# A four-layer graph network kernel: where the next block's rows of x are loaded, which PSUM bank its transposes use, and when dense blocks may start

## The reference

```
edge_index = stack([src, dst])
x = _layernorm(x + _L0(x, edge_attr_16, src, dst, W1, W2, attn, bias))
x = _layernorm(x + _L1(x, edge_index, edge_weight, ...))
x = _layernorm(x + _L2(x, edge_index, W, b))
x = _layernorm(x + _L3(x, src, dst, edge_weight, 100000))

_L1:  e = exp(scores - seg_max[dst]); att = e / segment_sum(e, dst)[dst]
      out = segment_sum(att * (alpha * phys + (1 - alpha) * neur), dst)
      h = _layernorm(gelu(out) + x, ln1_g, ln1_b)
      m = gelu(h @ mlp_w1.T + mlp_b1) @ mlp_w2.T + mlp_b2
      return _layernorm(m + h, ln2_g, ln2_b)
_L3:  y = segment_sum(value[:, None] * x[col], row)
```

## Time and profile before

| | us |
|---|---|
| time, median of 3 runs | 3338.48 (3337.09 to 3351.1) |
| the profiled execution: its own time | 3352.47 |
| its span | 3350.7 |
| PE, DVE, ACT, POOL busy | 2159.2, 1627.2, 1632.0, 2055.5 |

### The profile page before, as it was taken

One profiled execution on the slowest core, in us unless ns is written; L12 is line 12 of the kernel. 1 busy time (PEld: TensorE's weight loads), 2 busy tenths in 40 slices (PEclk: granted clock), 3 DMA queues, 4 the chain that ended last, 5 costly groups with the idle time before them and its releaser, 6 DMA issues. The chain is left out here.

```text
span 3350.7 us, 28393 instructions
## 1 busy us (share of the span) xinstructions
PE 2159.2 (64%) x9124; PEld 1081.8 (32%) x9124; DVE 1627.2 (49%) x3065; ACT 1632.0 (49%) x2292; POOL 2055.5 (61%) x1609
## 2 busy tenths in 40 slices
PE   6885777687787888888885744778777730012221
PEld 3432333265333336334333633333332210001210
DVE  5873899837878673443332676332233310012221
ACT  4763566434677672777773333656567720001110
POOL 6888888600488810466657888688800048788887
PEclk9997898769999896999997656888899965555555
DMA  2221222106322211244347342111111101112221
GB/s 57 63 67 43 54 56 53 48 21 191 89 46 43 43 37 47 79 104 106 105 102 160 82 110 69 44 37 38 37 52 38 38 23 14 14 31 57 62 56 26
DMA packets 251594, 204.24 MB, mean 61 GB/s; under 512 B 182627, under 2 KB 192167, under 8 KB 251446
## 3 DMA queue, kind: packets, MB, share of 16 engines
q1 hardware_dynamic: 164998, 154.80, 16.3%
q0 software_dynamic: 83200, 47.29, 8.7%
q10 hardware_dynamic: 3248, 0.34, 0.1%
HBM read 133.83 MB, written 79.64 MB: 64 GB/s over the span
## 5 line engine op out<-in xcount | busy, mean ns | idle before, releaser
L810 PE MATMUL ps<-wk 127*64 127x125 f32 x1200 | 121.0, 367 | 559.0 <-DVE wk L795 558.0
L2172 POOL DMA_INDIRECT stab<-wk,rank_i x200 | 243.1, 1215 | 313.5 <-issue 247.8
L483 ACT ACTIVATE b_s<-ps,vec 128x512 f32<-128x512 f32 (+1 forms) x444 | 297.1, 682 | 125.7 <-PE ps L480 71.4
L2169 POOL DMA_INDIRECT u<-x2tab,dpos_i x200 | 278.0, 1390 | 79.6 <-issue 77.8
L2169 POOL DMA_INDIRECT u<-x3tab,src_i x200 | 258.4, 1292 | 72.3 <-issue 72.3
L2169 POOL DMA_INDIRECT u<-in_x_dram,dst_i x200 | 263.9, 1320 | 61.0 <-issue 57.6
L2169 POOL DMA_INDIRECT u<-in_x_dram,src_i x200 | 249.3, 1246 | 73.5 <-issue 69.2
L810 PEld LDWEIGHTS ps<-wk 127*64 127x64 f32 x1200 | 96.3, 191 | 580.7 <-DVE wk L795 576.7
L2172 POOL DMA_INDIRECT out_dram<-e_c,dst_i x72 | 89.4, 1242 | 309.2 <-issue 309.2
L840 ACT ACTIVATE e_a<-ps 128x500 f32<-128x500 f32 x75 | 44.0, 586 | 456.7 <-PE ps L810 452.3
L2169 POOL DMA_INDIRECT e_b<-x0tab,dpos_i x72 | 91.7, 1274 | 244.0 <-issue 244.0
(11 more groups left out here) (416 smaller groups left out, 5653.5 us busy)
## 6 DMA issues: line engine op xcount, KB each, us to landing
b_s<-in_x_dram SPq DMA_DIRECT2D x98, 256.0 KB
out_dram<-b_gl SPq DMA_DIRECT2D x98, 256.0 KB
wk<-dlist SPq DMA_DIRECT2D x50, 500.0 KB
wk<-slist SPq DMA_DIRECT2D x50, 500.0 KB
u<-stab SPq DMA_DIRECT2D x25, 510.0 KB
x2none<-b_gl SPq DMA_DIRECT2D x25, 250.0 KB
wk<-x2none SPq DMA_DIRECT2D x25, 240.0 KB
x2tab<-wk SPq DMA_DIRECT2D x25, 240.0 KB
```

The lines of the kernel that those rows point to most:

```text
L483: return nc.scalar.activation(b_s[l][:, 0:w], (pA, pB)[n][l][:, 0:w], ACT.Abs_reciprocal_sqrt, bias=col(EPSV))
L810: last_a = nc.tensor.matmul(e0[64 * (k % 2):64 * (k % 2) + 64, P * (k // 2):P * (k // 2) + P], msg[n % 2][0:P + 2, D * k:D * k + D], sr[n ...
L2169: pool.indirect_dma_start(out=o, out_offset=None, in_=tab, in_offset=at(ix), **kw).then_inc(s, 16)
L2172: pool.indirect_dma_start(out=tab, out_offset=at(ix), in_=a, in_offset=None, bounds_check=rows_n - 1, oob_is_err=False).then_inc(s, 16)
```

## The change

It has four parts. (1) The load of a dense block's rows of x goes to columns 512 to 1023 of the gelu buffer, and waits for the `w2` matmuls of the job before it on the lane (`mlp_pe{l}`), no longer for that job's `rows`. (2) The head of every job changes banks: `t` transposes into `pB`, `u` reads `pB`, the centred rows stand in `pA`, and the mean of squares in `pB`. `t` waits for the last reciprocal root of the job before (`rstds{l}`), `u` or `x` for its `rows` (`rows_ps{l}`), and the first matmul into `pA` for its `out` (`rows_out{l}`). In the plan the lane is given back at `r5` (dense) or `r4` (`src`, `dst`), no longer at `out`. (3) The plan starts no dense block while one of two spans is open: from the first `u3` step to the first `src` head, and from `lay` 1's step `b10` to the head of `dst` group 2. (4) The planner also counts loads of ScalarE's table for the reciprocal root, prefers a step that needs no new table among those ready at the same time, and counts an engine's slowness and table load when it chooses between ACT and DVE for `u` and `out`.

```diff
-            unit(("src", g), 1, "t pe .5 +lane;x act 1.2;s pe 2.2;r act .7;h dve .9;" + MLP + "rows pe .5;out act|dve .7 -lane",
+            unit(("src", g), 1, "t pe .5 +lane;x act 1.2;s pe 2.2;r act .7;h dve .9;" + LAST_MLP + "rows pe .5;out act|dve .7",
...
-                 "sq5 act .75;j5 pe 1.2;r5 act .7;o dve .75;rows pe .5;out act|dve .7 -lane", [(("dense", n - 1), "t", 0)] if n else ())
+                 "sq5 act .75;j5 pe 1.2;r5 act .7 -lane;o dve .75;rows pe .5;out act|dve .7", [(("dense", n - 1), "t", 0)] if n else ())
...
-        TABLES = {"gelu": 1, "g": 1, "exp": 2}
+        TABLES = {"gelu": 1, "g": 1, "exp": 2, "r": 3, "r3": 3, "r4": 3, "r5": 3, "rs": 3, "rst": 3}
...
-        GRACE = .2
+        GRACE, X_IN, SAME_TABLE = .1, 6.0, 0.0
+        HOLD = ((("u3", 0, "t"), ("src", 0, "t")), (("lay", 1, "b10"), ("dst", 2, "t")))
...
+                        if key[0] == "dense" and any(a in end and z not in end for a, z in HOLD):
+                            t = 1e6
...
 dense_pe
             if m:
-                pe.wait_ge(S(f"rows_out{l}"), m)
+                pe.wait_ge(S(f"rstds{l}"), c)
...
-                last_t = nc.tensor.transpose(pA[l][:, 128 * q:128 * q + 128], b_s[l][:, 128 * q:128 * q + 128], ident[:, :])
+                last_t = nc.tensor.transpose(pB[l][:, 128 * q:128 * q + 128], b_gl[l][:, 512 + 128 * q:640 + 128 * q], ident[:, :])
...
             pe.wait_ge(S(f"head_u{l}"), before(l, m, dense=1) + 1)
-            nc.tensor.matmul(pB[l], blk_c[:, :], b_h[l][:, :], start=True, stop=True).then_inc(S(f"head_c{l}"), 1)
+            if m:
+                pe.wait_ge(S(f"rows_out{l}"), m)
+            nc.tensor.matmul(pA[l], blk_c[:, :], b_h[l][:, :], start=True, stop=True).then_inc(S(f"head_c{l}"), 1)
...
 dense_sp
-            yield max(t["t"] - 6, lane_jobs[l][m - 1][0]["rows"] + 1.2 if m else 0)
+            yield lane_jobs[l][m - 1][0]["w2"] + 2.4 if m else t["t"] - 6
             if m:
-                sp.wait_ge(S(f"rows_ps{l}"), m)
-            sp.dma_start(b_s[l][:, :], x[dense_row(n):dense_row(n) + NB, :].rearrange("(p t) d -> p (t d)", p=128)).then_inc(
+                sp.wait_ge(S(f"mlp_pe{l}"), 3 * m - 1)
...
+            sp.dma_start(b_gl[l][:, 512:1024], x[dense_row(n):dense_row(n) + NB, :].rearrange("(p t) d -> p (t d)", p=128)).then_inc(
                 S(f"x_in{l}"), 16)
```

More of the change, by code:

```diff
@@ L191, in unit @@
             order.append(key)
[L193 to L194 removed]
+        MLP = ("w1 pe 1.3;gelu act 1.1;w2 pe 2.1;sq3 act .7;j3 pe 1.2;r3 act .7;mt dve .75;d pe 1.2;v dve .75;sq4 act .65;"
+               "j4 pe 1.2;r4 act .7{};x2 dve .7;")
+        LAST_MLP = MLP.format(" -lane")
+        MLP = MLP.format("")
         LANDED, STORED, EDGES_IN = 1.8, 4.5, 5.0
@@ L257, in gnn_resnorm_kernel @@
             sums_unit(NG + g, "msg dve 1.4;same dve 1.2;t pe .5 +lane;x act .6;a pe 2.2;ag act 1;o pe 1.2;g act .6;c pe 2.3;sq act .7;"
-                      "j pe 1.2;r act .7;h dve .75;" + MLP + "rows pe .5;out dve 1.3 -lane",
+                      "j pe 1.2;r act .7;h dve .75;" + LAST_MLP + "rows pe .5;out dve 1.3",
                       [(("lay", 1), "copy", CARRIED if g == 0 else 0)] + [(("xd1", g), "mul", 0)],
@@ L351, in make_plan, with lane_at, slow, switch @@
                     open_if(key, name)
+            def lane_at(l, key):
+                return max(lane_free[l], x_free[l] if key[0] == "dense" else 0.0)
+            def slow(eng, t):
+                return next((f for a, z, f in BUSY if a <= t < z), 1.0) if eng == "dve" else 1.0
+            def switch(eng, name):
+                return 1.28 if eng == "act" and TABLES.get(name, table[0]) != table[0] else 0.0
             def start(eng, key, name):
@@ L373, in make_plan @@
                     first = min(c[0] for c in cand)
-                    pick = min((units[s_[0]]["rank"], t, s_, eng) for t, s_ in cand if t <= first + GRACE)
+                    wait = max(GRACE, SAME_TABLE) if eng == "act" else GRACE
+                    pick = min((switch(eng, s_[1]), t > first + GRACE, units[s_[0]]["rank"], t, s_, eng)
+                               for t, s_ in cand if t <= first + wait)[2:]
                     if best is None or pick[1] < best[1]:
@@ L378, in make_plan @@
                 _, engs, us, takes, gives, _ = units[key]["steps"][name]
-                on[key[0], key[1], name] = eng
-                if eng == "dve":
-                    us *= next((f for a, z, f in BUSY if a <= t < z), 1.0)
-                if eng == "act" and TABLES.get(name, 0) != table[0]:
-                    table[0] = TABLES.get(name, 0)
-                    us += 1.28
+                on[key][name] = eng
+                if "|" not in engs:
+                    us = us * slow(eng, t) + switch(eng, name)
+                if eng == "act":
+                    table[0] = TABLES.get(name, table[0])
                 for e in engs.split("|"):
@@ L394, in make_plan @@
                     if r == "lane":
-                        l = min(LANES, key=lambda k: max(lane_free[k], lane_rows[k] + 6 if key[0] == "dense" else 0.0))
+                        l = min(LANES, key=lambda k: lane_at(k, key))
                         lane_of[key] = l
                         jobs[l].append((key, t))
-                        lane_free[l] = 1e9
+                        lane_free[l] = x_free[l] = 1e9
+                        names_ = list(units[key]["steps"])
+                        names_ = names_[names_.index("t"):]
+                        for k, p in ((1, "rows"), (2, "out")):
+                            if last[l] and (last[l], p) not in end:
+                                left[key, names_[k]] += 1
+                                then.setdefault((last[l], p), []).append((key, names_[k], 0.0))
+                        last[l] = key
                     else:
@@ L402, in make_plan @@
                         spare[r] = 1e9
-                if name == "rows" and key in lane_of:
-                    lane_rows[lane_of[key]] = done
+                if name == "w2":
+                    x_free[lane_of[key]] = done + X_IN
                 for r in gives:
@@ L560, in dense_act @@
             rstd(l, 512)
-            nc.scalar.activation(b_gl[l][:, 512:1024], pA[l], ACT.Abs_reciprocal_sqrt, bias=col(EPS2),
+            nc.scalar.activation(b_gl[l][:, 512:1024], pB[l], ACT.Abs_reciprocal_sqrt, bias=col(EPS2),
                                  scale=1.0 + EPS).then_inc(S(f"rstds{l}"), 1)
@@ L570, in dense_act @@
                                  scale=1.0 + EPS).then_inc(S(f"rstds{l}"), 1)
-            if on["dense", n, "out"] == "act":
+            if o["out"] == "act":
                 yield t["out"]
@@ L590, in dense_dve @@
                                            ALU.mult).then_inc(S(f"dense_o{l}"), 1)
-            if on["dense", n, "out"] == "dve":
+            if o["out"] == "dve":
                 yield t["out"]
@@ L656, in src_dve @@
             yield from mlp_dve(dve, t, l, m, c + 1, EW)
-            if on["src", g, "out"] == "dve":
+            if o["out"] == "dve":
                 yield t["out"]
```

96 lines of the change are left out of this document (57 added, 39 removed).

## The result

| | median us | ratio to before, 95% interval |
|---|---|---|
| before, timed beside it | 3344.79 (3337.09 to 3353.3) | |
| changed | 3196.6 (3189.67 to 3202.78) | 0.9556 [0.952, 0.9591] |

The changed kernel is 148 us faster where 111 were forecast. The time lies in the range of 3196 to 3278, but only 0.6 us above its lower end. That is less than the spread of the kernel's own runs. The median of before is 6 us above the 3338.48 from which the forecast started, and the ratio applied to that number gives 3190. The profiled execution took 3202.78 us, and its span is 3201.0, so 149.7 less than before's span.

What follows compares the result with a forecast made beforehand. The span was taken as `u6`'s end (2437.1) plus 285.2 us of dense work plus 628.4 us of POOL scatters. Tail -125.8 and +15 ahead gave -111, from 3338.48 to 3227.5 us; range 3196 to 3278.

Steps and rivals of the forecast that it cites:

- Ten heads behind `u6`, and the tail: Dense work after `u6`: 10 heads remain instead of 19, tail 159.4 us instead of 285.2, so -125.8 us.
- The rate: Dense tail: 12.5 us a block instead of 13.2, with ends 13.2 and 10.8; 12 to 13 would show it.
- with the gap closed PE becomes the limit: Dense tail: without the lane's 7.2 us gap a block takes PE's own work, 10.8 us if fully packed.
- The 87% packing of the best stage: Dense tail: PE won't be packed fully, as best stages reach 85% and 87%; 10.8 / 0.865 = 12.5 us a block.
- Rival A: Dense tail: ACT, not PE, is the next limit at 9.7 us a block; 3199 us; chance 0.08.
- The cost of nine blocks ahead: Stages up to `u6`'s end: nine more blocks there move that end by +15 us, bounds +3 to above +45.
- the 2440 to 2480 that should have shown it: Sign in the trace after: `u6`'s last matmul stands at 2440 to 2480 us.
- The mis-sized term: `dst` stage, 1366 to 1765: earlier lane hand-over packs PE better, taken as -10 us; 90% packing would give 22 less.
- the forecast's 12: Gap ahead of `u4`, 1190 to 1366: one more block in sum, 10.8 / 0.87 = +12 us.
- Each dense block put ahead of `u6`'s end for nothing shortens it.: Whole span: `u6`'s end plus 285.2 us dense work plus 628.4 us scatters; blocks moved ahead free shorten it.
- Rival E: SP's in-order queue: the new load's wait holds up `dst` groups; at 8 us each +200, 3428 us; chance 0.04.
- No wait of `gelu` for a store: `gelu` overwriting `b_gl`: store is free some 5.6 us after `r5`, 6.8 us remain, so costed at nothing.

Runs made afterwards that it cites:

- e7: Changed kernel with one more 128x512 matmul on TensorE in step `j5` of each of the last ten blocks; 3204.46 us.
- e8: Changed kernel with ScalarE's Square of step `sq5` done twice in each of the last ten blocks; 3203.91 us.
- e10: Changed kernel with two tiny activations in ten of the 25 `dst` groups, forcing 20 more ScalarE table loads; 3230.37 us, ratio 0.9671.
- e11: Changed kernel without the planner's preference for a step that needs no new table; loads still counted; 3189.73 us, ratio 0.9535.
- e4: Kernel before with part 1 (the load) alone; 3246.23 us, ratio 0.9698.
- e3: Changed kernel with before's plan costs and no holds, so parts 1 and 2 only; 3198.82 us, ratio 0.9554.
- e9: Changed kernel replanned with no holds and every dense block ahead, so no heads behind `u6`; 3197.33 us, ratio 0.9563.
- e2: Changed kernel without the two holds (part 3); 3191.73 us, ratio 0.9536.
- e6: Changed kernel without part 4, holds kept; 3216.0 us, ratio 0.9606.
- e12: Changed kernel with the preference for a loaded table only from `lay` 1's step `b10` on; 3166.38 us, ratio 0.9475.

## Why the prediction came out as it did

**Ten heads behind `u6`, and the tail.** Right. 19 x 13.2 + 34.4 became 10 x 11.56 + 37.7. Of the 131.8 us, 9 x 13.2 = 119 are the heads that are gone, 10 x (13.2 - 11.56) = 16 the rate, and -3 the drain. Of those 3 us, 0.9 are the matmul of the last block's mean of squares, which took 2.07 us instead of 1.13, at the lower clock.

**The rate.** The number was near (12.5 forecast, 11.56 measured, inside its ends, but below the 12 to 13 that should have shown it). The step behind it, "with the gap closed PE becomes the limit", holds by half. e7 says that TensorE passes on 0.63 of an added 0.86 us, e8 that ScalarE passes on 0.56 of 0.77. So PE is one of two engines that carry the rate, and not the limit by itself. The 87% packing of the best stage, by which I raised 10.8 to 12.5, was no ceiling: the `dst` stage now packs to 91%. The chain of a lane, which explained the 13.2, would have given a better number. From head to head a block took (2687.9 - 2448.0) / 18 = 13.3 us before and (2535.0 - 2433.7) / 9 = 11.3 after, so a lane's turn went from 40.0 to 33.8 us, 6.2 less, and the mean hand-over from 7.6 to 0.5, 7.1 less. Most of what the hand-over saved arrives in the rate.

**Rival A's rule.** PE has 123.86 us in the tail. 10 blocks begin there and 13 end, 11.5 blocks' worth and 10.8 us a block, as before. So a denser queue doesn't squeeze busy PE, which was what A needed. The Trainium skill (Perfetto Trace Analysis, Identifying the Most-Contended Engine) says that matmul busy time is not a good measure of how close a kernel is to roofline, and that the share of weight loads should be used. Weight loads are busy for 43.72 of 153.4 us here, which would leave TensorE much room; e7 found little, since an added matmul cost three quarters of the time that it takes.

**The cost of nine blocks ahead.** This is the step that failed: +15 us on `u6`'s end forecast, -17.7 measured (2437.1 to 2419.4), outside the bounds of +3 to +45 and ahead of the 2440 to 2480 that should have shown it. Term by term:

| stage | forecast | measured |
|---|---|---|
| 0 to 650 | 0 | +5.3 |
| gap ahead of `u3` | +13 | +6.3 |
| `u3` | 0 | -0.5 |
| gap ahead of `u4` | +12 | +0.5 |
| `dst` stage | -10 | -32.4 |
| `u5`, `u6` | 0 | +3.1 |

The mis-sized term is the `dst` stage, and in it Part 4, which I costed at 0 for the choice of engine and didn't look at for the order of ScalarE's steps. The trace of before would have shown it: 87 loads of 1.28 us stand in that stage. e10 and e11 show that they are paid for there. But part 4 gave only 17 of the 32 us; 10 came with the load alone (e4) and 5 more with the banks and the hand-over (e3). Why the load shortens a stage whose groups load no rows of x stays open. The two gaps came out cheaper than forecast. The one ahead of `u3` has 9 heads in it instead of 6 in the traces and is only 6.3 us longer. The one ahead of `u4` took its fifth head for 0.5 us, but beyond that two more cost 21 us (e11), four more 50 (e3) and five more 76 (e9), 11 to 15 a block. So the forecast's 12 is right as a mean for the later ones, and the fifth came free.

**"Each dense block put ahead of `u6`'s end for nothing shortens it."** True with the stress on "for nothing". e3 has six heads fewer behind than the changed kernel and the same time, e9 has ten fewer and the same time. What the blocks saved in the tail they cost ahead of it.

**Other terms.** The scatters took 628.2 us. Rival E did not come: SP stood in front of the load for less, not more, as this row of SP's waits in the changed kernel says beside the earlier trace rows (774.6, 49, 68.3):

```profile
SPq L639 <- PE ps L496: 657.0, 89, 65.9
```

"No wait of `gelu` for a store" was wrong, at no cost. The changed kernel's timeline has one; here are the store and the wait:

```profile
1750.40 0.36 SPq L646 DMA_DIRECT2D out_dram<-b_gl  x1
...
1775.79 1.28 ACT L517 ACT_TABLE_LOAD   x1 [12.54 <-DMA out_dram<-b_gl]
```

There are three such waits from 1400 to 2100 us, 19.6 us in all. I had priced a store at the 3.1 us of an idle queue. The table load waits for the semaphore that the store issued at 1750.40 raises, so from that issue to ScalarE's next instruction pass 25.4 us, eight times as many. The DMA engines are busy for 99% of those 25 us, mostly with the loads of the edge groups' records (`stab`) that SP issues around it; 42% is only the mean of the stretch. POOL sets the time there, and the time shows no loss from the wait.

**Part 3** was costed at 0 and measures 0 beside part 4 (e2), but +17 us without it (e6 against e3). What an edit to an order costs depends here on the other edits.

## What to carry to other kernels

Cut the span where the engine that sets the time changes, and ask of each piece of movable work what it costs in the stretch it goes to: the 11.6 us that a block saved behind `u6` were 11 to 15 in the gaps and near nothing beside POOL's passes. To learn which engine carries a rate, add one step to each in turn, and count from the first added step on: the stretch ahead of it varies by itself. In a stage whose busiest engine is at 85 to 91%, work on another engine at 76% can still be paid for in full, as ScalarE's table loads were in the `dst` stage. When a planner's rule gains in one stage, try it in that stage alone; here that was worth about 30 us more than the rule everywhere.

## What the runs showed of the hardware

A change of ScalarE's table takes 1.28 us on ScalarE in these traces. Two rows of the changed kernel's timeline around one:

```profile
2477.62 1.28 ACT L517 ACT_TABLE_LOAD   x1
...
2478.91 1.11 ACT L517 ACTIVATE b_gl<-ps,vec 128x1024 f32<-128x1024 f32 x1
```

The activation starts 1.29 us after the load's start. Of the changed kernel's 305 loads, 302 start within 0.02 us of the end of the instruction before, and 279 have the next activation within 1.30 us of their own start. The Trainium skill (ScalarE: Activation LUTs, What ACT_TABLE_LOAD costs) gives 1.28 us for the load, which agrees, and a drain of 1.38 us beside it, 2.66 in all, which these traces don't show. What a load more cost the `dst` stage was 0.6 us where the order was planned with it (e11) and 1.7 where it was not (e10, each with an activation of 0.18 us and a wait for it).

TensorE's granted clock in the `dst` stage was 0.97 before, 1.00 in the changed kernel, in e11 and in e12, and 0.96 in e10. 1.00 is the higher of its two levels, 2.4 GHz, all the way; in the others it stood at the lower one, 1.2 GHz, for a small part of the stage. How much of the stage's 32 us, and of e10's 33, is the clock's was not measured apart.
